# Dealing router steps and turns over other units of the 16-expert stages, and starting the second 8-expert stage's low rows earlier

## The chip, the cores and the metric

The kernel runs on one core of a Trainium2 chip. The metric is the device time of one execution in microseconds (us); the median of the runs is compared. Engines: PE (TensorE), DVE (VectorE), ACT (ScalarE), POOL (GpSimd), SP (SyncE, which here only issues DMAs).

## The reference

A stack of six blocks on a residual `x` of 8 sequences x 512 tokens x 128 features, float32:

```python
x = x + 0.5 * _L0_ffn_ref(_layernorm(x), ...)   # 8 experts, hidden 512, top 2
x = x + _L0_attn_ref(_layernorm(x), ...)        # 16 heads of 8
x = x + 0.5 * _L0_ffn_ref(_layernorm(x), ...)
x = x + 0.5 * _L1_ffn_ref(_layernorm(x), ...)   # 16 experts, width 64, top 2, and a shared one
x = x + _L1_attn_ref(_layernorm(x), ...)        # a state space block
x = x + 0.5 * _L1_ffn_ref(_layernorm(x), ...)
```

The part that matters here, the 16-expert block, is

```python
shared_out = silu(x @ shared_gate_w) * (x @ shared_up_w) @ shared_down_w
topk_probs, topk_idx = top_k(softmax(x_flat @ router_w), 2)
coeff = einsum('tk,tke->te', topk_probs, one_hot(topk_idx, 16))
for g, u, d, c in experts:
    acc = acc + (silu(x_flat @ g) * (x_flat @ u)) @ d * c[:, None]
```

The 8-expert block is a gelu layer pair per expert, weighed by the two largest probabilities of a softmax router.

## The kernel before, in words

Six phases run one after the other (`PHASES`: moe0, attn, moe0, moe1, ssm, moe1). There is no scheduler: each phase has one function per engine (`tensor`, `scalar`, `vector`, `gpsimd`, `sync`), and the order on an engine is the order in which that function issues. Engines meet by semaphores alone (`wait_ge`), and every engine runs its own instructions strictly in order, so an instruction that waits holds all behind it.

**The 16-expert stage** (`moe1_phase`). One body per sequence, `b` from `c0` to `end - 1`, eight in a stage. A body has nine units `j`: unit 0 is the shared expert, units 1 to 8 are pairs of routed experts. For a unit PE does two products of three matmuls each (`up1`, L1590 to L1592: high weights x high rows, high x low, low x high), ACT the silu (`silu1`, L1645), DVE the gate product (`gate1`, L1654 for unit 0 and L1657) and, four units later (`W_LAG`), the weighing with the token's coefficient (`weigh1`, L1666); PE's down product (`down1`, L1678) comes six units behind (`D_LAG`) and sums over the units in bank 6. Three units may be open between PE and DVE (`UPS`): PE starts a unit only when the gate three units back is done.

Beside the units a body prepares the next ones:

- the turn `norm_pe` (L231): PE transposes the normed rows of a later sequence into bank 7, and `norm_act` (L237) copies them to `xnT`; `xh_act` (L1596) and `xl_dve` (L1600) split `xnT` into high and low rows;
- the router: `router_pe` (L1507), then on DVE `router_a` (5 short operations, L1520 to L1525), `router_b` (7, L1533 to L1541) and `router_c` (7, L1549 to L1559), `router_b` and `router_c` each in two halves where the code wants them apart; ACT's `router_act` (tanh, L1512) stands between;
- the coefficients: `coef_pe` (L1565) transposes them into bank 7, `coef_act` (L1571) copies them to SBUF, and SP (`coef_sp`) stores them and loads them back repeated over 64 partitions, four loads of 512 KB, into one of two buffers;
- `arrive`: DVE brings sequence b + 2 up to date, by `combine` in the first stage (L313, eight operations: the routed rows of the 8-expert stage) and by a shorter update in the second (L3034); then `norm_a` (L204, L209) takes its statistics, POOL finishes them (`shift_pool`), and ACT writes the normed rows (`xn_act`, L1613);
- `back_pe` (L1692) transposes the sum of body b - 1 into bank 7 and `back_dve` (L1697) adds it to `x_res`.

Bank 7 is shared by turn, router, coefficients and `back_pe`; the turn at a body's end waits for L1697. The body `c0 + 1` differs: the coefficients of `c0` land late, so the down products of `c0` are made in its first units (`FIRST_DOWNS`, L1678) and DVE weighs two units of `c0` behind each of its first four gates.

**The second 8-expert stage** (`moe0_phase`, `occ` 1). The first sequence is computed densely, expert by expert: `i` is the expert, `c` one of four units (`up0` L950 to L952, `gelu0` L1014, `hh_act` L1024, `hl_dve` L1034, `down0`), `y_act`, `back_pe` (L1053) and `y_dve` (L1062, the weighed add to `x_res`) behind it; `back_pe(i)` needs `y_dve(i - 1)`. Meanwhile the last group of routed tokens gets its slots: `pick_a`, `pick_b` (L529 to L550), `group_pos` on PE, `group_copy` on ACT, `place_a`, `place_b` (L587 to L617), `place_c` (L626 to L636), `tables_dve`. The `route_last_*` functions say at which (i, c) each stands. The rows of the first sequence come split: `xh_act` (L895) and `xl_dve` (L900). Both ran at the stage's opening, behind the attention's last add `z_dve` (L2427), and `after_phases` held PE for that add.

## Time and profile before

| | us |
|---|---|
| median of 3 runs (1391.99 to 1400.24) | 1392.63 |
| the profiled execution | 1398.67 |
| its span on the core | 1396.9 |
| PE busy | 1236.2 (88%) |
| DVE busy | 1123.6 (80%) |
| ACT busy | 876.3 (63%) |
| POOL busy | 513.5 (37%) |

All times of rows are microseconds from the span's start. In the span the second 8-expert stage begins near 704, the first 16-expert stage near 897, its third body near 946, the second 16-expert stage near 1202. PE's busy share is an average over stages; what an edit is worth is read from who waits for whom inside a stage. PEclk is the granted TensorE clock as a share of the full 2.4 GHz.

### The profile page before, as it was taken

How to read it: one execution, taken by the hardware profiler on the slowest of the kernel's cores; microseconds unless marked ns; L12 is line 12 of the kernel's file. 1: busy time of each engine (PE TensorE's matmuls, PEld its weight loads, DVE VectorE, ACT ScalarE, POOL GpSimd, SP SyncE). 2: the span in 40 equal slices, each digit the busy share in tenths (PEclk: the TensorE clock that was granted, in tenths of full speed). 3: DMA queues.
4: the chain of work that ended last, by engine and by line, in shares of the span. 5: the costliest groups of instructions: out<-in, count | busy, mean ns of one | idle time of the engine just before them, and what ended most of it. 6: DMA issues, size and time to landing. Idle time of an engine off the chain costs nothing.

```text
span 1396.9 us, 22511 instructions
## 1 busy us (share of the span) xinstructions
PE 1236.2 (88%) x7168; PEld 783.7 (56%) x7168; DVE 1123.6 (80%) x2387; ACT 876.3 (63%) x1535; POOL 513.5 (37%) x762
## 2 busy tenths in 40 slices
PE   6768999678899879988888999899999899899998
PEld 5657989312222212322277999866666356666665
DVE  6865979789988989898677989877876787778785
ACT  5855777358887868877887777633333588333442
POOL 6772337543543506520363236605330320210100
PEclk9988999679998989999999999999999999999999
DMA  7495556522212202210253566456363010253534
GB/s 267 131 357 179 204 203 227 159 70 79 90 48 84 86 26 96 89 44 13 78 225 126 188 222 217 139 113 142 84 130 70 11 42 19 52 121 73 116 69 121
DMA packets 116608, 167.94 MB, mean 120 GB/s; under 512 B 18884, under 2 KB 63460, under 8 KB 115468
## 3 DMA queue, kind: packets, MB, share of 16 engines
q1 hardware_dynamic: 109324, 151.82, 36.7%
q0 software_dynamic: 7168, 14.69, 3.6%
q8 instruction: 58, 0.95, 0.3%
q14 instruction: 58, 0.48, 0.1%
HBM read 80.72 MB, written 45.09 MB: 90 GB/s over the span
## 4 chain that ended last, share of the span: by engine, by line
PE 53%; DVE 25%; issue 8%; ACT 7%; DMA 4%; POOL 2%; SPq 1%; DVEq 0%; ACTq 0%; POOLq 0%
PE bank L1678 6%; DVE shared L2297 6%; PE bank L2375 5%; PE pair L950 4%; PE pair L952 4%; PE pair L951 4%; PE pair L2357 3%; PE pair L1590 3%; PE pair L1592 3%; PE pair L1591 3%; PE pair L2289 3%; DVE shared L1034 3%; DMA shared<-p_coef_rows 2%; ACT shared L2365 2%; DVE shared L1032 2%
## 5 line engine op out<-in xcount | busy, mean ns | idle before, releaser
L2297 DVE TENSOR_REDUCE shared<-pair 128x2 f32<-128x1024 f32 x256 | 309.8, 1217 | 40.7 <-PE pair L2289 37.8
L2365 ACT ACTIVATE shared<-pair 128x1024 f32<-128x1024 f32 x256 | 260.5, 1021 | 51.1 <-PE pair L2357 49.5
L950 PE MATMUL pair<-shared 128*128 128x256 f32 (+1 forms) x704 | 228.0, 324 | 7.1 <-issue 3.6
L951 PE MATMUL pair<-shared 128*128 128x256 f32 (+1 forms) x704 | 218.2, 310 | 0.0
L952 PE MATMUL pair<-shared 128*128 128x256 f32 (+1 forms) x704 | 218.0, 310 | 0.0
L1034 DVE TENSOR_TENSOR shared<-shared 128x512 fp32r<-128x512 f32 x208 | 155.7, 757 | 59.9 <-ACT shared L1024 56.7
L1645 ACT ACTIVATE shared<-pair 128x512 f32<-128x512 f32 x144 | 85.7, 595 | 180.9 <-PE pair L1592 180.8
L1590 PE MATMUL pair<-shared 128*128 128x512 f32 x288 | 154.6, 537 | 4.9 <-DVE shared L1600 4.9
L1018 ACT ACTIVATE shared<-pair,shared 128x256 f32<-128x256 f32 x288 | 121.3, 476 | 49.9 <-PE pair L952 43.5
L950 PEld LDWEIGHTS pair<-shared 128*128 128x128 f32 x704 | 137.8, 196 | 14.9 <-issue 4.5
L2375 PE MATMUL bank<-shared 128*9 128x512 f32 x1024 | 138.8, 615 | 4.5 <-ACT shared L2365 4.3
L952 PEld LDWEIGHTS pair<-shared 128*128 128x128 f32 x704 | 137.9, 196 | 6.4
L1333 POOL CAST shared<-shared 128x1024 fp32r x72 | 81.6, 1134 | 161.7 <-PE pair L952 150.7
L951 PEld LDWEIGHTS pair<-shared 128*128 128x128 f32 x704 | 137.6, 196 | 5.4 <-issue 0.2
L649 POOL DMA_INDIRECT xs_rows<-shared,slots x112 | 117.6, 1050 | 55.5 <-issue 28.7
L281 POOL DMA_INDIRECT staged<-ys_rows,slots x112 | 116.3, 1039 | 57.1 <-ACT shared L2365 34.0
L1657 DVE TENSOR_TENSOR shared<-shared,pair 128x512 f32<-128x512 f32 x128 | 87.0, 682 | 58.6 <-ACT shared L1645 57.1
L1678 PE MATMUL bank<-shared,down_w 128*128 128x512 f32 x256 | 128.7, 595 | 1.6 <-DVE shared L1666 1.6
L2289 PE MATMUL pair<-shared 48*128 48x512 bf16 x512 | 104.2, 406 | 22.2 <-ACT shared L2365 10.5
L1592 PE MATMUL pair<-shared 128*128 128x512 f32 x288 | 115.4, 401 | 0.0
L1591 PE MATMUL pair<-shared 128*128 128x512 f32 x288 | 115.1, 400 | 0.0
L2357 PEld LDWEIGHTS pair<-shared 51*128 51x128 bf16 x512 | 24.7, 93 | 150.0 <-issue 88.6
(384 smaller groups left out, 2253.4 us busy)
## 6 DMA issues: line engine op xcount, KB each, us to landing
shared<-shared SPq DMA_DIRECT2D x144, 256.0 KB
shared<-p_coef_rows SPq DMA_DIRECT2D x64, 512.0 KB, 6.4
shared<-xs_rows SPq DMA_DIRECT2D x36, 256.0 KB, 3.0
ys_rows<-shared SPq DMA_DIRECT2D x36, 256.0 KB
w_keep<-shared SPq DMA_DIRECT2D x8, 1024.0 KB, 12.2
shared<-w_keep SPq DMA_DIRECT2D x16, 512.0 KB
shared<-p_q_parts SPq DMA_DIRECT2D x64, 96.0 KB, 2.3
shared<-p_k_parts SPq DMA_DIRECT2D x64, 96.0 KB, 2.4
```

What stands on the lines that cost most here:

```text
L950: nc.tensor.matmul(out_bank, w_hi, x_hi, start=start, stop=False)
L951: nc.tensor.matmul(out_bank, w_hi, x_lo, start=False, stop=False)
L952: return nc.tensor.matmul(out_bank, w_lo, x_hi, start=False, stop=stop)
L1034: nc.vector.tensor_tensor(hl[u % RING][:], hid[u % RING][:], hh[u % RING][:], ALU.subtract).then_inc(s["dve_done"], 1)
L1590: nc.tensor.matmul(out_bank, w_hi, x_hi, start=start, stop=False)
L1591: nc.tensor.matmul(out_bank, w_hi, x_lo, start=False, stop=False)
L1592: return nc.tensor.matmul(out_bank, w_lo, x_hi, start=False, stop=stop)
L1678: nc.tensor.matmul(bank[6][:], w, h, start=(j == 0), stop=(j == IT - 1)).then_inc(s["down_done"], 1)
L2289: last = nc.tensor.matmul(pair_of("max", b, m)[:, f, :], qa[par][rows, c, i * P:(i + 1) * P], ka[par][rows, c, :], start=True, stop=True)
L2297: nc.vector.tensor_reduce(mneg[:, i, 2 * c:2 * c + 2], pair_of("max", b, m)[:], AX_X, ALU.max, negate=True).then_inc(s["mx_read"], 1)
L2365: nc.scalar.activation(probs[st % 2][:, 2 * p:2 * p + 2, :], pair_of("exp", b, 2 * st + p)[:], ACT.Exp, scale=scale).then_inc(s["exp_done" ...
L2375: last = nc.tensor.matmul(bank[6][32 * hh:32 * hh + HD + 1, :], v_all[:, b * TILES + kt, hh % 2 * (H // 2) + g * HG // 2 + hh // 2, :], pr ...
```

## The change

It adds and removes no computation. Six moves:

1. Bodies from the third on: the turn `norm_pe`/`norm_act` goes from the end of body b - 1 (unit 8) and the head of body b to behind unit 1 of body b; the router matmuls from unit 0 to unit 2, `router_act` from 2 to 3, `router_a`, `router_b`, `router_c` from units 1, 2, 3 to 2, 3, 4.
2. The second body (`late`): everything of item 1 a unit later, except `router_c`, which stays at unit 4, now with `router_b`; `arrive` goes from unit 4 to unit 5.
3. First body: `router_b` and `router_c`, which stood together at unit 5, are dealt in halves to units 5, 6, 7, 8, and the low rows go from unit 7 to unit 6.
4. The coefficients of the second body are transposed and copied in its own unit 1 (on ACT ahead of that unit's silu) instead of at unit 8 of the first.
5. Second 8-expert stage: the low rows of the first sequence get a place in SBUF behind all others, and both halves of the split go into the attention's last steps: `xh_act` ahead of `ot_act`, `xl_dve` between `place_a` and `place_b`, ahead of `z_dve`. PE no longer calls `after_phases`.
6. Second 8-expert stage: the last group's slot work is dealt over units: `pick_a` (2,3), `pick_b` (3,0), positions (3,3), `place_a` in halves at (3,3) and (4,0), `place_b` in halves at (4,0) and (4,1), `place_c` in halves at (4,2) and (4,3).

The core of the diff:

```diff
             if occ:
                 w_all = view(P, NE0 * 4 * HID, F32R)
+                low_rows = view(P, T, F32R)
+            xl = [low_rows, low_more]
...
+            if occ:
+                dense_open.update(xh=lambda: xh_act(0), xl=lambda v: xl_dve(v, 0))
...
+            def last_group(v, G, at):
+                if at == (2, 3):
+                    pick_a(v, occ, G)
+                if at == (3, 0):
+                    pick_b(v, occ, G)
+                if at == (3, 3):
+                    place_a(v, occ, G, 0)
+                if at == (4, 0):
+                    place_a(v, occ, G, 1)
+                    place_b(v, occ, G, 0)
+                if at == (4, 1):
+                    place_b(v, occ, G, 1)
...
             def tensor(t):
-                after_phases(t, n)
                 f = base(n + 1)
                 if occ == 0:
+                    after_phases(t, n)
...
-                            if j == 8:
-                                coef_pe(b + 1)
                             continue
...
-                        if j == 1 and b == c0 + 1:
-                            nc.tensor.wait_ge(s["ct_sb"], b + 1)
+                        late = int(b == c0 + 1)
+                        if j == 1 and late:
+                            coef_pe(b)
+                        if j == 1 + late and ahead(b - 1):
+                            if b == c0 + 1:
+                                nc.tensor.wait_ge(s["ct_sb"], b + 1)
+                            else:
+                                nc.tensor.wait_ge(x_upd, u0 + b - 1)
                             norm_pe(f0 + b + 1)
-                        if j == (2 if b == c0 + 1 else 0) and b + 1 < end:
+                        if j == 2 + late and b + 1 < end:
                             router_pe(b + 1)
...
-                        if j == 8 and ahead(b):
-                            nc.tensor.wait_ge(x_upd, u0 + b)
-                            norm_pe(f0 + b + 2)
...
                         else:
-                            if j == 0 and b > c0 + 1 and ahead(b - 1):
-                                norm_act(f0 + b + 1, (b + 1) % 2)
+                            if j == 1 and b == c0 + 1:
+                                coef_act(b)
...
                             if j == 5:
-                                router_b(chain)
-                                router_c(v, b + 1, chain)
-                            if j == 7:
+                                router_b1(chain)
+                            if j == 6:
                                 xl_dve(v, b + 1)
+                                router_b2(chain)
+                            if j == 7:
+                                router_c1(v, b + 1, chain)
+                            if j == 8:
+                                router_c2(v, b + 1, chain)
...
-                        if j == (4 if b > c0 else 3) and b + 2 < end and not (mixed(n) and b == c0):
+                        if j == (4 if b > c0 + 1 else 5 if b > c0 else 3) and b + 2 < end and not (mixed(n) and b == c0):
                             arrive(v, b + 2 - c0)
```

The order of the changed kernel carries other line numbers: L1600, L1657, L1654, L1678, L1565 and L1590 of before are L1625, L1682, L1679, L1703, L1590 and L1615 in it.

DVE in the first body of a 16-expert stage, before, from the last router step of unit 5 to the first gate of the second body (`coef` holds the coefficients, `stats` and `mv` the statistics, L1600 writes the low rows):

```order
L1559 SCALAR_TENSOR_TENSOR coef<-rt_b,rt_m 128x64
L1657 TENSOR_TENSOR shared<-shared,pair 128x512
L204 BN_STATS stats<-x_res 128x6 x4
L209 BN_AGGR mv<-stats 128x2 x4
L1657 TENSOR_TENSOR shared<-shared,pair 128x512
L1600 TENSOR_TENSOR shared<-xnT,shared 128x512
L1657 TENSOR_TENSOR shared<-shared,pair 128x512
L1654 SCALAR_TENSOR_TENSOR shared<-shared,pair 128x512
```

and with the change, from unit 6's gate on:

```order
L1682 TENSOR_TENSOR shared<-shared,pair 128x512
L1625 TENSOR_TENSOR shared<-xnT,shared 128x512
L1563 TENSOR_TENSOR rt_a<-rt_a,first 128x64
L1564 TENSOR_REDUCE rt_n<-rt_a 128x4
L1565 TENSOR_TENSOR rt_a<-rt_a,rt_n 128x64
L1566 TENSOR_TENSOR rt_c<-rt_a,rt_c 128x64
L204 BN_STATS stats<-x_res 128x6 x4
L209 BN_AGGR mv<-stats 128x2 x4
L1682 TENSOR_TENSOR shared<-shared,pair 128x512
L1574 TENSOR_SCALAR rt_b<-rt_th 128x64
L1575 RECIPROCAL rt_b<-rt_b 128x64
L1576 SCALAR_TENSOR_TENSOR rt_b<-rt_th,rt_b 128x64
```

The low rows (L1600, now L1625) went from behind unit 7's gate to behind unit 6's, and the router steps that had all stood ahead of unit 6's gate now lie between the gates of units 6, 7 and 8.

PE at the seam of the second and third body, before: the last down product of the second, the turn (`xn`), unit 0 of the third, the router matmuls (`wr`, `xnT`) behind it.

```order
L1678 MATMUL bank<-shared,down_w 128x512
L231 MATMUL bank<-ident,xn 128x128 x4
L1590 MATMUL pair<-shared 128x512
L1591 MATMUL pair<-shared 128x512
L1592 MATMUL pair<-shared 128x512
L1590 MATMUL pair<-shared 128x512
L1591 MATMUL pair<-shared 128x512
L1592 MATMUL pair<-shared 128x512
L1678 MATMUL bank<-shared,down_w 128x512
L1507 MATMUL bank<-wr,xnT 128x16 x4
```

With the change, unit 1 of the third body with the down product ahead of it and behind it, and then the turn:

```order
L1703 MATMUL bank<-shared,down_w 128x512
L1615 MATMUL pair<-shared 128x512
L1616 MATMUL pair<-shared 128x512
L1617 MATMUL pair<-shared 128x512
L1615 MATMUL pair<-shared 128x512
L1616 MATMUL pair<-shared 128x512
L1617 MATMUL pair<-shared 128x512
L1703 MATMUL bank<-shared,down_w 128x512
L231 MATMUL bank<-ident,xn 128x128 x4
```

The turn left the body's end and stands two units later; the router matmuls follow another unit later.

DVE in the dense part of the second 8-expert stage, before, around the weighed add of the second expert (L1062):

```order
L616 TENSOR_REDUCE slot_f<-q_g 128x4
L617 CAST slots<-slot_f 128x8
L1034 TENSOR_TENSOR shared<-shared 128x512 x2
L626 SCALAR_TENSOR_TENSOR moved_e<-rest_e,jump_e 128x8
L627 TENSOR_TENSOR next_e<-next_e,pos_g 128x8
L628 TENSOR_TENSOR next_e<-next_e,moved_e 128x8
L629 SCALAR_TENSOR_TENSOR room_e<-blocks_e,rest_e 128x8
L632 TENSOR_TENSOR past_e<-upto_e,iota 128x288
L634 TENSOR_REDUCE ex_g<-past_e 128x36
L635 SCALAR_TENSOR_TENSOR ex_g<-ex_g 128x36
L636 TENSOR_TENSOR ex_all<-ex_all,ex_g 128x36
L1062 SCALAR_TENSOR_TENSOR x_res<-bank,w_dense,x_res 128x128 x4
```

and with the change:

```order
L1039 TENSOR_TENSOR shared<-shared 128x512
L626 SCALAR_TENSOR_TENSOR moved_e<-rest_e,jump_e 128x8
L627 TENSOR_TENSOR next_e<-next_e,pos_g 128x8
L628 TENSOR_TENSOR next_e<-next_e,moved_e 128x8
L629 SCALAR_TENSOR_TENSOR room_e<-blocks_e,rest_e 128x8
L1039 TENSOR_TENSOR shared<-shared 128x512
L632 TENSOR_TENSOR past_e<-upto_e,iota 128x288
L634 TENSOR_REDUCE ex_g<-past_e 128x36
L635 SCALAR_TENSOR_TENSOR ex_g<-ex_g 128x36
L636 TENSOR_TENSOR ex_all<-ex_all,ex_g 128x36
L1067 SCALAR_TENSOR_TENSOR x_res<-bank,w_dense,x_res 128x128 x4
L1039 TENSOR_TENSOR shared<-shared 128x512 x2
```

The low halves of two units now lie inside the slot work instead of beside it; the weighed add (now L1067) still comes behind all of it.

## Rows read from the trace of the kernel before

**Rows 1.** The page, its first line.

```profile
span 1396.9 us, 22511 instructions
```

**Rows 2.** Waits of PE, 896 to 1066: us in total, times, longest.

```profile
PE bank L231 <- DVE x_res L1697: 7.9, 5, 1.8
PE pair L1590 <- DVE shared L1600: 2.4, 1, 2.4
```

**Rows 3.** Busy time by stretch: PE, PEld, DVE, ACT, POOL, PEclk, DMA share, GB/s.

```profile
962.92:987.00 24.08, 22.55 (x93) 15.44 (x92) 19.50 (x56) 9.32 (x18) 10.69 (x12) 1.00 0.50 111
968.00:970.00 2.00, 0.47 (x3) 0.07 (x2) 1.40 (x3) 1.78 (x5) 1.63 (x2) 1.00 0.90 210
1224.00:1228.00 4.00, 3.88 (x10) 3.12 (x11) 0.95 (x3) 0.91 (x3) 1.16 (x2) 0.57 0.08 19
1268.62:1291.53 22.91, 22.56 (x93) 15.44 (x92) 18.36 (x51) 9.32 (x18) 2.04 (x4) 1.00 0.45 94
```

**Rows 4.** Order of time at two body seams, first 16-expert stage: start, us, engine.

```profile
945.88 0.63 PE L231 MATMUL bank<-ident,xn 128*128 128x128 f32 x4 [1.77 <-DVE x_res L1697]
...
966.32 0.68 DVE L1666 TENSOR_TENSOR shared<-shared 128x512 f32<-128x512 f32 x1
...
967.41 1.02 PE L1678 MATMUL bank<-shared,down_w 128*128 128x512 f32 x2
969.96 0.63 PE L231 MATMUL bank<-ident,xn 128*128 128x128 f32 x4 [1.53 <-DVE x_res L1697]
970.35 0.48 PE L1590 MATMUL pair<-shared 128*128 128x512 f32 x1
```

**Rows 5.** Order of time on DVE in the body that begins at 970.35.

```profile
972.63 0.69 DVE L1654 SCALAR_TENSOR_TENSOR shared<-shared,pair 128x512 f32<-128x512 f32 x1 [0.96 <-ACT shared L1645]
...
975.77 0.69 DVE L1657 TENSOR_TENSOR shared<-shared,pair 128x512 f32<-128x512 f32 x1 [1.85 <-ACT shared L1645]
...
985.01 2.31 DVE L313 SCALAR_TENSOR_TENSOR x_res<-staged,w_tok,x_res 128x128 f32<-128x128 f32 x8
```

**Rows 6.** First two bodies of that stage: DVE, ACT, PE in time; coefficient loads.

```profile
910.98 0.69 DVE L1657 TENSOR_TENSOR shared<-shared,pair 128x512 f32<-128x512 f32 x1 [0.51 <-ACT shared L1645]
...
916.11 0.57 ACT L1571 COPY shared<-bank 16x512 f32<-16x512 f32 x1 [0.23 <-PE bank L1565]
...
918.37 0.68 DVE L1657 TENSOR_TENSOR shared<-shared,pair 128x512 f32<-128x512 f32 x1
918.50 0.50 PE L1590 MATMUL pair<-shared 128*128 128x512 f32 x1 [2.43 <-DVE shared L1600]
...
921.45 1.28 DVE L1666 TENSOR_TENSOR shared<-shared 128x512 f32<-128x512 f32 x2
922.18 1.98 PE L1678 MATMUL bank<-shared,down_w 128*128 128x512 f32 x4 [0.63 <-DVE shared L1666]
922.25 0.58 ACT L1645 ACTIVATE shared<-pair 128x512 f32<-128x512 f32 x1
...
shared<-p_coef_rows SPq DMA_DIRECT2D x4, 512.0 KB, 6.1
```

**Rows 7.** Second 8-expert stage: PE, ACT and DVE in order of time.

```profile
703.74 0.47 PE L950 MATMUL pair<-shared 128*128 128x512 f32 x1 [2.67 <-DVE x_res L2427]
704.77 1.28 ACT L1014 ACT_TABLE_LOAD   x1 [4.50 <-PE pair L952]
...
724.32 0.18 DVE L529 TENSOR_REDUCE mx_g<-z_all 128x4 f32<-128x32 f32 x1
...
727.35 0.19 PE L508 MATMUL bank<-summed_g,ones_b 128*128 128x32 bf16 x1 [0.35 <-DVE summed_g L550]
...
738.73 1.13 DVE L1062 SCALAR_TENSOR_TENSOR x_res<-bank,w_dense,x_res 128x128 f32<-128x128 f32 x4
...
740.00 1.09 PE L1053 MATMUL bank<-ident,shared 128*128 128x128 f32 x4 [3.52 <-DVE x_res L1062]
```

59 lines of the change are left out of this document (34 added, 25 removed).

## The prediction

> **What bounds the kernel now.** I read the waits of TensorE (PE) stage by stage first, then PE's busy time in one body, then the order of time on PE, VectorE (DVE) and ScalarE (ACT) around each wait. In the first 16-expert stage the rows to see are five waits of PE for the residual add L1697, 7.9 us in all, and one of 2.4 us for the low rows L1600 [rows 2]. A steady body there lasts 24.08 us with PE busy 22.55; in the second 16-expert stage it lasts 22.91 with the same 22.56 busy [rows 3]. So PE is the bound in both, and the 1.5 us between them is the turn L231 at the body's end waiting for L1697: 1.53 us [rows 4]. DVE is busy 19.50 of 24.08, but in a lump: from unit 1's gate at 975.77, which still waited 1.85, it has no gap to the end of the combine at 987.32 [rows 5]. The second 8-expert stage starts at 703.74 after 2.67 us of waiting and loses 3.52 us at 740.00, where a transpose waits for the add L1062 that DVE reaches at 738.73 [rows 7].
>
> The profiled execution took 1398.67 us around its span of 1396.9 [rows 1], 6.0 over the median of 1392.63; I sum savings in the trace and take them off the median.
>
> **Steady bodies of the first 16-expert stage.** No instruction is added or removed; the turn goes behind unit 1 of the next body, so L1697 has some 4.5 us more, and the 1.53 goes. What is late next is DVE. Before, its lump begins with unit 1's gate, 975.77-970.35 = 5.42 us into the body. Now router part a goes with unit 2, b with 3, c with 4. Unit 2's gate can begin at 5.42 + 2.25 (a unit with its down product: 22.55 us over nine units, less turns and router) - 0.81 (router matmuls now behind it) + 0.39 (the turn now ahead) = 7.25. From there the old lump, less unit 1's gate and weighing (1.2), is 11.55-1.2 = 10.35, and unit 3's gate, which must wait for 7.25+2.25+0.81 = 10.31 while DVE is ready at 7.25+1.2+1.3 = 9.75, puts 0.55 into it: the combine ends at 18.15, not at 987.32-970.35 = 16.97. DVE is 1.2 us later for the weighings behind it. The tightest is the one at 966.32, ended 966.95, whose product PE began at 967.41 [rows 4]: slack 0.46, plus 0.39 because the turn now stands ahead of PE too, 0.85. So a wait of about 0.35 comes back: 24.08-1.53+0.35 = 22.9, a saving of 1.2 in each of four bodies (third to sixth), **4.8 us**. Bounds: nothing (the whole 1.5 comes back) to 1.55 a body, 6.2.
>
> **First two bodies of that stage.** Before, DVE does router parts b and c in one piece after unit 5's gate (910.98), so that the low rows end late and PE's second body starts at 918.50, after 2.43 [rows 6]. Now the low rows stand right behind unit 6's gate, near 913, and this wait goes. But all that DVE had to do before unit 8's gate (918.37) is still to be done, c2 now behind it. The second body's first gate comes at 918.37+0.65 = 919.0 and its first weighing at 919.6, 1.85 before the old 921.45. PE's down product, which began 0.73 behind that weighing (922.18), begins at 920.35: the 2.4 has moved there, and 1.85 is won. Next, on ACT the coefficient copy is now queued ahead of unit 1's silu, and on PE the coefficient transposes stand behind two down products (1.7): they end at 922.45, the copy at 923.2, the silu starts then, where it was 922.25 before, and the next weighing is ready for PE at 923.2+0.6+0.6+0.75 = 925.15. PE has done unit 2 by 922.45+1.45 = 923.9 and waits 1.25: 0.6 of the gain is left. From 925.15 PE needs two downs, turn, unit 3, two downs, router, unit 4 (7.5 us) and the silu 0.85, so unit 4's gate is at 933.5. Behind it DVE now has b and c together (3.7), gate and weighing (1.2), combine (2.3), statistics (1.3), gate and weighing (1.2): 943.2, ready for PE some 0.7 later, 943.9. PE has come to that product at 942.5 and waits 1.4. It ends near 944.8, and the third body starts there without the turn that began at 945.88 before [rows 4]: **1.1 us** won. Bounds: -3 (the three waits of 2.4, 1.3 and 1.4 hold and each also loses clock) to +4.8 (2.4, 0.6 and 1.8, all gone). I take the path just worked, since each wait in it is read from neighbours.
>
> The coefficients of the second body leave 6.5 us later than before (copy 916.11, now 922.7). The four loads land 6.1 us after issue [rows 6]; with the store before them that is some 9 to 13 us, so 932 to 936, and their first user runs after 937: hidden, with 1 us to spare.
>
> **The second 16-expert stage.** The same two bodies, with a 1.2 us update in place of the combine. The same steps give PE's first down product at 1225.9 (before 1229.06), then waits of 1.3 and 0.4, and the third body 2.4 us earlier; of this 1.5 is clock, since behind its 2.42 us wait the granted clock was 0.57 for 4 us [rows 3], the 1.2 GHz level for much of it. The four steady bodies can fall only from 22.91 to some 22.5, DVE having 1.1 us less to do: 1.6. Together **4.0 us**, bounds 0 and 7.
>
> **The second 8-expert stage.** PE no longer waits for the attention's last add; low rows written between the two halves of slot work let it start near 701.1. But ACT still waits for that add, which the low rows push 0.7 later, to 703.65, so the first gelu (table load at 704.77 before) comes 1.1 earlier, not 2.6. Downstream DVE decides. Its pick (724.32 before) starts 2.1 earlier, with one unit less ahead of it: PE now meets its result one unit sooner and waits there some 1.5 (0.35 before). From the pick to L1062 at 738.73 [rows 7] DVE had almost no gap, and dealing the same instructions out removes none: the add ends 0.75 earlier. The early start is thus swallowed at 740: **0.75 us**. Bounds: -0.7 (the add later by the low rows) and +6.6 (2.7, 3.5 and 0.4). The reloads of weights start 0.7 later and stay ahead of use.
>
> **Sum.** 4.8 + 1.1 + 4.0 + 0.75 = 10.65. 1392.63 - 10.65 = 1382.0 us, 0.76% less. A measurement of this kernel tells about 1% (13.9 us) from no change.
>
> **Rivals.**
> *All the named waits go and nothing takes their place.* 11.3 in the first 16-expert stage, 5 and 1.5 of clock in the second, 6.7 in the 8-expert one: 24.5, so 1368.1. For it: DVE and ACT have room on average. Against: DVE's lump is continuous just where the waits are [rows 5, 6].
> *The wait comes back in the steady bodies.* If DVE's slack is half a microsecond smaller than I read, each steady body of the first stage keeps 1.2 to 1.5 as waits on weighings; only the rest is won: 1392.63 - 5.85 = 1386.8. For it: the combine, statistics and weighings stand in a row. Against: DVE has 24.08 - 19.50 = 4.6 us of gaps in a body [rows 3] to catch up.
> *The clock falls: slower than before.* Waits of PE that were one per body become several short ones, in four steady bodies and three in each second body: ten. Behind 2.42 us of waiting the clock was 0.57 for 4 us, which cost 1.7 [rows 3]. Ten times that is 17, against 10.65: 1399. It decides from seven of the ten on. Against: behind 1.53 us waits the clock stayed at 1.00, the 2.4 GHz level, in the stretch 968 to 970 too [rows 3].
> The Trainium skill ("TensorE: Matmul & The Clock Gate", section "A second HAM failure mode: psum-queue depth-cycling") says that frequent short idles between groups of matmuls can make the clock swing between its levels. By it this rival would hold and the time be near 1399; the trace has short idles at full clock, so it gets little.
> *The change does nothing it says.* Excluded for the turn, which moves in every body; for the 8-expert stage it is my own forecast, nearly.
>
> **How the numbers follow.** Forecast, with a few microseconds either way (1377 to 1386): 0.52. Steady waits back (1384 to 1390): 0.20. All waits gone or mostly (1366 to 1377): 0.23. Clock: 0.05. Leaving out one in ten at either end, 1372 to 1389. Faster by over 1% needs 13.9 us: the 0.23 and a little of the forecast's edge, 0.26. Slower by over 1%: 0.02. Within: 0.72.
>
> **What would show it.** In the changed profile the turn L231 waits nowhere; steady bodies of the first stage last 22.9, with down products waiting 0.3 to 0.5 for weighings; in each second body PE waits 2.3 for the first weighing, about 1.3 for the third, 1.4 (0.4 in the second stage) for the last; in the 8-expert stage a wait of 1.5 at the group positions and one of 2.8 for L1062's successor, ending near 739. It would be wrong if the second body's waits were missing, if the steady body lasted over 23.5, or if the 8-expert stage gained over 2 us.

## The result, and the profile after

| | before | changed |
|---|---|---|
| median of six runs, us | 1395.64 (1391.99 to 1400.24) | 1382.64 (1379.44 to 1385.08) |
| ratio, 95% interval | | 0.9918 (0.9895 to 0.994) |
| profiled execution's span, us | 1396.9 | 1379.8 |

The change makes the kernel 0.82% faster, and the whole interval lies below 1; the forecast was 0.76%. The spans differ by more than the medians, 17.1 us. Of these, 5.5 lie ahead of the change, in stages that it does not touch: the attention's output product starts at 699.93 in the trace before and at 694.47 in the changed one, and in a later run with those stages unaltered too (the 16-expert parts alone) at 695.18. So the two traces are compared stage by stage, each from its own first mark: A from the attention's output product to the coefficient transposes of the first 16-expert stage (it holds the second 8-expert stage), B from there to that stage's last transposes back (L1717, before L1692), S the state-space stage up to the next coefficient transposes, C from there to the last transposes back.

| us | A | B | S | C |
|---|---|---|---|---|
| before | 197.3 | 195.0 | 117.3 | 183.2 |
| changed | 194.1 | 189.3 | 118.3 | 179.5 |
| gained | 3.2 | 5.7 | -1.0 | 3.7 |
| forecast | 0.75 | 5.9 | 0 | 4.0 |

The sum is 11.7, beside 11.4 by the ratio and 13.0 by the medians.

One caution for B. PE runs unaltered code in the stage's first units, but its granted clock over the first 5 us was 0.50 in the trace before and 0.71 in the changed one. The kernel with the 16-expert parts alone, below, started at 0.50 as well and took 190.5 us in B. So at the same starting clock B gains 4.5, and 1.2 of the 5.7 is that clock.

The waits of TensorE in the changed kernel, first for 890 to 1066 (it answers to [rows 2]), then for 1190 to the end:

```profile
PE bank L1703 <- DVE shared L1691: 4.5, 3, 2.1
...
PE bank L1703 <- DVE shared L1691: 3.5, 3, 2.1
PE bank L1590 <- DVE coef L1584: 1.6, 1, 1.6
PE bank L1717 <- ACT shared L1707: 0.7, 1, 0.7
```

The turn L231 no longer waits for the residual add, and the 2.4 us for the low rows is gone. In their place stand waits of the down product L1703 (L1678 before) for the weighing L1691: three in the second body of the first stage, two in that of the second stage (2.08 and 1.08; the third counted in that line, 0.29, is at the stage's very last products). The wait for the coefficients L1584, 1.6, ends just where C begins and so is counted in S. Busy time in the body that begins at each turn, two of the first 16-expert stage and one of the second, to be read beside [rows 3]:

```profile
939.66:962.83 23.17, 23.07 (x94) 15.39 (x92) 19.41 (x55) 9.20 (x18) 10.31 (x12) 1.00 0.49 105
962.83:985.99 23.16, 23.05 (x93) 15.39 (x92) 19.41 (x55) 9.20 (x18) 10.30 (x12) 1.00 0.53 118
...
1263.26:1285.67 22.41, 22.41 (x94) 15.53 (x93) 18.34 (x51) 9.20 (x18) 2.03 (x4) 1.00 0.47 101
```

A body went from 24.08 to 23.16 and from 22.91 to 22.41. The busy column misleads here: PE shows 23.05 busy of 23.16, though its work is the same 22.41 as in the second stage. A matmul's end is modelled, and a short wait hides under it. What shows such waits is the weight load's row (PEld), which names whom it waited for, and the distance of each matmul from the body's start, laid beside the same matmul of the stage without waits:

```profile
974.23 2.31 DVE L313 SCALAR_TENSOR_TENSOR x_res<-staged,w_tok,x_res 128x128 f32<-128x128 f32 x8
976.57 0.69 DVE L1682 TENSOR_TENSOR shared<-shared,pair 128x512 f32<-128x512 f32 x1
977.18 0.68 DVE L1691 TENSOR_TENSOR shared<-shared 128x512 f32<-128x512 f32 x1
977.91 0.30 PEld L1703 LDWEIGHTS bank<-shared,down_w 128*128 128x128 f32 x2 [0.34 <-DVE shared L1691]
980.35 0.30 PEld L1703 LDWEIGHTS bank<-shared,down_w 128*128 128x128 f32 x2 [0.37 <-DVE shared L1691]
980.96 0.19 PEld L1615 LDWEIGHTS pair<-shared 128*128 128x128 f32 x1 [0.31 <-DVE shared L1625]
981.52 1.65 ACT L1638 ACTIVATE xn<-x_res,shift,rs_y 128x128 f32<-128x128 f32 x4 [3.52 <-POOL shift L1632]
983.08 1.06 ACT L1670 ACTIVATE shared<-pair 128x512 f32<-128x512 f32 x2
985.03 0.30 PEld L1703 LDWEIGHTS bank<-shared,down_w 128*128 128x128 f32 x2 [0.34 <-DVE shared L1691]
```

Against the second stage's body, PE falls behind by 0.38 us at the weighing behind the combine (977.91), by 0.10 and 0.14 at 980.35 and at the low rows (980.96), and, after 0.05 is made up, by 0.18 from 985.03 on: 0.75 in all, the whole difference of 23.16 and 22.41.

The second body of the first 16-expert stage, in order of time (answers to [rows 6]):

```profile
908.83 0.68 DVE L1679 SCALAR_TENSOR_TENSOR shared<-shared,pair 128x512 f32<-128x512 f32 x1
909.42 1.28 DVE L1691 TENSOR_TENSOR shared<-shared 128x512 f32<-128x512 f32 x2
910.16 1.98 PE L1703 MATMUL bank<-shared,down_w 128*128 128x512 f32 x4 [2.07 <-DVE shared L1691]
...
911.98 0.60 PE L1590 MATMUL bank<-ident,coef 128*16 128x128 f32 x4
...
912.62 0.58 ACT L1596 COPY shared<-bank 16x512 f32<-16x512 f32 x1 [2.96 <-PE bank L1590]
913.10 0.58 ACT L1670 ACTIVATE shared<-pair 128x512 f32<-128x512 f32 x1
...
914.32 1.29 DVE L1691 TENSOR_TENSOR shared<-shared 128x512 f32<-128x512 f32 x2
915.06 1.12 PE L1703 MATMUL bank<-shared,down_w 128*128 128x512 f32 x2 [1.10 <-DVE shared L1691]
...
934.04 0.70 PE L1703 MATMUL bank<-shared,down_w 128*128 128x512 f32 x1 [1.30 <-DVE shared L1691]
```

These are the three waits that were forecast as 2.3, 1.3 and 1.4: the first weighing behind VectorE's lag, the third behind the silu that is queued after the coefficient copy, the last behind router, combine and statistics. In the second stage the third of them shows only in the weight load's row, and PE falls behind by 0.46 us there:

```profile
1235.25 0.30 PEld L1703 LDWEIGHTS bank<-shared,down_w 128*128 128x128 f32 x2 [0.57 <-DVE shared L1691]
```

The second 8-expert stage (answers to [rows 7]):

```profile
695.36 0.48 PE L955 MATMUL pair<-shared 128*128 128x512 f32 x1
...
696.40 1.28 ACT L1019 ACT_TABLE_LOAD   x1 [2.07 <-PE pair L957]
...
697.37 0.69 DVE L2456 TENSOR_TENSOR x_res<-bank,shared 128x512 f32<-128x512 f32 x1
...
698.09 1.27 ACT L1019 ACTIVATE shared<-pair,vecs 128x512 f32<-128x512 f32 x2 [0.41 <-DVE x_res L2456]
...
718.86 0.19 PE L508 MATMUL bank<-summed_g,ones_b 128*128 128x32 bf16 x1 [1.26 <-DVE summed_g L550]
...
731.09 1.13 DVE L1067 SCALAR_TENSOR_TENSOR x_res<-bank,w_dense,x_res 128x128 f32<-128x128 f32 x4
732.36 0.63 PE L1058 MATMUL bank<-ident,shared 128*128 128x128 f32 x4 [2.48 <-DVE x_res L1067]
```

From the attention's output product the first gelu is 3.62 us away (698.09 - 694.47), before it was 6.14; the stall at L1058 ends 37.9 us away, before 40.1. It lasts 2.48 instead of 3.52, and the wait at the group positions grew from 0.35 to 1.26.

### The profile page after: what moved, and what is told of

The parts are those of the page before. It is cut to its first block, busy times and chain, and to the rows that moved or that the text cites. A ratio compares the mean times of both kernels' runs of the same rounds, so it can differ in the third digit from the quotient of the medians.

```text
span 1379.8 us, 22519 instructions
## 1 busy us (share of the span) xinstructions
PE 1227.8 (89%) x7168; PEld 776.2 (56%) x7168; DVE 1120.5 (81%) x2387; ACT 875.9 (63%) x1535; POOL 511.8 (37%) x762
## 4 chain that ended last, share of the span: by engine, by line
PE 54%; DVE 25%; issue 8%; ACT 8%; POOL 3%; DMA 2%; SPq 0%; DVEq 0%; ACTq 0%; POOLq 0%
PE bank L1703 8%; DVE shared L2326 6%; PE bank L2404 5%; PE pair L1615 4%; PE pair L1617 4%; PE pair L1616 3%; PE pair L955 3%; PE pair L957 3%; PE pair L2386 3%; PE pair L956 3%; PE pair L2318 3%; DVE shared L1039 3%; ACT shared L2394 2%; POOL xs_rows L649 2%; DVE shared L1037 2%
## 5 line engine op out<-in xcount | busy, mean ns | idle before, releaser
L2326 DVE TENSOR_REDUCE shared<-pair 128x2 f32<-128x1024 f32 x256 | 309.9, 1217 | 37.9 <-PE pair L2318 34.8
L955 PE MATMUL pair<-shared 128*128 128x256 f32 (+1 forms) x704 | 225.5, 320 | 6.8 <-issue 3.6
L957 PE MATMUL pair<-shared 128*128 128x256 f32 (+1 forms) x704 | 215.9, 307 | 0.0
L956 PE MATMUL pair<-shared 128*128 128x256 f32 (+1 forms) x704 | 215.6, 306 | 0.0
L1615 PE MATMUL pair<-shared 128*128 128x512 f32 x288 | 152.4, 529 | 0.2 <-DVE shared L1625 0.2
L955 PEld LDWEIGHTS pair<-shared 128*128 128x128 f32 x704 | 136.0, 193 | 15.0 <-issue 5.4
L1682 DVE TENSOR_TENSOR shared<-shared,pair 128x512 f32<-128x512 f32 x128 | 87.2, 682 | 65.9 <-ACT shared L1670 64.8
L957 PEld LDWEIGHTS pair<-shared 128*128 128x128 f32 x704 | 135.8, 193 | 5.9
L956 PEld LDWEIGHTS pair<-shared 128*128 128x128 f32 x704 | 135.7, 193 | 4.9 <-issue 0.2
L1703 PE MATMUL bank<-shared,down_w 128*128 128x512 f32 x256 | 130.4, 601 | 8.8 <-DVE shared L1691 8.2
L649 POOL DMA_INDIRECT xs_rows<-shared,slots x112 | 117.6, 1050 | 51.4 <-issue 28.9
L2318 PE MATMUL pair<-shared 48*128 48x512 bf16 x512 | 103.6, 403 | 22.5 <-ACT shared L2394 10.8
L1617 PE MATMUL pair<-shared 128*128 128x512 f32 x288 | 114.2, 397 | 0.0
L1616 PE MATMUL pair<-shared 128*128 128x512 f32 x288 | 113.7, 395 | 0.0
```

Source lines behind the costliest of these rows:

```text
L649: g.indirect_dma_start(out=xs_rows, out_offset=bass.IndirectOffsetOnAxis(ap=slots[:, t, k:k + 1], axis=0), in_=xn_rows[occ][:, t, :], in_o ...
L955: nc.tensor.matmul(out_bank, w_hi, x_hi, start=start, stop=False)
L956: nc.tensor.matmul(out_bank, w_hi, x_lo, start=False, stop=False)
L957: return nc.tensor.matmul(out_bank, w_lo, x_hi, start=False, stop=stop)
L1615: nc.tensor.matmul(out_bank, w_hi, x_hi, start=start, stop=False)
L1616: nc.tensor.matmul(out_bank, w_hi, x_lo, start=False, stop=False)
```

## The experiments

Stage lengths of all profiled runs, beside the medians; the last two columns are the granted clock over the first 4 us of A and the first 5 us of B (before: 1.00 and 0.50; changed: 1.00 and 0.71). Kernels of one group of lines shared their runs of the kernel before.

| kernel | median us | ratio to before | A | B | S | C | clock, A | clock, B |
|---|---|---|---|---|---|---|---|---|
| 8-expert part alone | 1389.59 | 0.9964 (0.9946 to 0.9982) | 193.9 | 194.8 | 117.0 | 182.7 | 1.00 | 0.70 |
| 16-expert parts alone | 1385.63 | 0.9942 (0.9922 to 0.9962) | 198.1 | 190.5 | 117.4 | 179.5 | 0.77 | 0.50 |
| early low rows alone | 1392.49 | 0.9992 (0.9972 to 1.0012) | 197.1 | 196.4 | 117.3 | 183.1 | 0.57 | 0.66 |
| low rows twice | 1384.77 | 0.994 (0.9916 to 0.9964) | 194.0 | 189.9 | 118.3 | 179.6 | 1.00 | 0.72 |
| | | | | | | | | |
| dealing alone | 1392.63 | 0.9984 (0.9965 to 1.0003) | 197.2 | 194.8 | 117.0 | 182.7 | 0.80 | 0.68 |
| low rows earlier | 1384.36 | 0.9934 (0.991 to 0.9957) | 194.6 | 190.5 | 117.1 | 179.5 | 1.00 | 0.53 |
| down products later | 1373.62 | 0.986 (0.9834 to 0.9887) | 194.5 | 185.9 | 114.1 | 176.2 | 1.00 | 0.51 |
| silu first | 1379.02 | 0.9887 (0.9863 to 0.9911) | 195.4 | 189.0 | 114.3 | 178.1 | 1.00 | 0.50 |
| | | | | | | | | |
| second body, three parts | 1376.51 | 0.9895 (0.9876 to 0.9914) | 194.8 | 184.7 | 117.0 | 175.7 | 0.54 | 0.66 |
| norm later | 1383.82 | 0.9936 (0.991 to 0.9961) | 194.1 | 188.4 | 117.2 | 179.6 | 1.00 | 0.72 |
| both | 1372.33 | 0.986 (0.9841 to 0.9879) | 194.1 | 183.5 | 117.6 | 175.8 | 1.00 | 0.71 |
| changed kernel again | 1381.08 | 0.9942 (0.9921 to 0.9963) | 195.2 | 189.3 | 118.3 | 179.5 | 0.57 | 0.72 |

**The two halves of the change.** The kernel before with the 8-expert part of the diff alone, then with the 16-expert part alone.

> The kernel before with the two parts of the change in the second 8-expert stage alone (low rows' home and early low rows, slot work dealt out); the 16-expert stages are as before. Theory (the stage's gain is its own and lasts): from the attention's last product to the 16-expert stage's coefficient transposes 3.2 us less than in the kernel before, its median 3 us lower, ratio 0.9977. Rival (the prediction's own step: the add on VectorE decides and swallows the early start, what the changed profile showed was the clock's luck): 0.75 us less.

> The kernel before with the change of the two 16-expert stages alone. Theory (the parts add up): first 16-expert stage 5.7 us shorter, second 3.8 us shorter, as in the changed kernel, median some 8.5 to 9.5 us lower, ratio 0.9936, since the 8-expert stage's 3.2 is missing. Rival (the parts lean on each other, for instance through the low rows' home or the time at which weights arrive): either stage differs from the changed kernel's by more than 1 us.

Measured: A 193.9 with the first, 198.1 without it (before: 197.3). B and C are 190.5 and 179.5 with the second, and B is 1.2 longer than in the changed kernel. That 1.2 arises in the stage's first 10 us, where PE runs unaltered code: the granted clock over the first 5 was 0.50 in this run, as in the kernel before, and 0.71 in the changed kernel's. The steady bodies are 23.17 and 22.41 as there. The ratios multiply to 0.9906, beside 0.9918 for the whole. So the parts add up, and the 8-expert part wins over 3 us, not 0.75; the rival of the first run falls, and that of the second is met by its number (over 1 us in B) but by the clock, not by the parts leaning on each other.

**Which half of the 8-expert part.** Early low rows alone:

```diff
-                dense_open["xT"] = xT_dense
+                dense_open.update(xT=xT_dense)
...
+                dense_open.update(xh=lambda: xh_act(0), xl=lambda v: xl_dve(v, 0))
```

with the low rows' own home, the calls in the attention's end and PE's entry without its wait as in the change; the last group's steps stay where they were.

> The kernel before with the early low rows (and their own home) alone; pick, placing and group positions of the last group stay in one piece and at their old units. Theory: the first up product comes 2.9 us earlier, the clock does not fall at 705, and the gain is kept but for what the undealt placing costs: 2 to 2.6 of the 3.2 us. Rival (the prediction's: VectorE's work up to the residual add decides, and only dealing could move it): the stall after that add grows from 3.5 us to 5.5, 0.75 us or less is won.

Then the dealing alone, low rows left behind the attention's add. (PE's call of `after_phases` is gone in this kernel too. PE then waits for the low rows instead, and its first product stands where it stood, 3.75 us behind the attention's output product against 3.81 before.)

> The kernel before with the dealing of the last group's slot work in the second 8-expert stage alone; low rows where they were. In the trace from the attention's last product to the 16-expert stage's coefficients the kernel before takes 197.3 us (198.1 in the run with the 16-expert parts alone), with low rows alone 197.1, with both parts 193.9. Theory (the dealing is what pays: it takes VectorE's work out from before the residual add, whose stall goes from 3.5 to 2.5, and the low rows only hand on their start): some 195.5. Rival (neither pays alone; the start of 2.9 us and the dealing are needed together): 197 or more. Rival of the prediction (dealing the same instructions out moves nothing): 197.3 and the stall at 3.5.

A is 197.1 and 197.2, where both together give 193.9 to 195.4 in ten profiles and neither gives 197.3 and 198.1 in two. By these figures neither pays alone, but they can't be laid side by side as they are. The stalls of PE at the transposes behind the weighed add, with low rows alone and with the dealing alone, each followed by the ten microseconds behind it (busy times, granted clock third from the right):

```profile
733.71 1.09 PE L1058 MATMUL bank<-ident,shared 128*128 128x128 f32 x4 [3.56 <-DVE x_res L1067]
...
733.71:743.71 10.00, 10.00 (x38) 8.02 (x39) 4.77 (x13) 3.98 (x7) 4.46 (x5) 0.71 0.28 89
```

```profile
735.79 0.63 PE L1053 MATMUL bank<-ident,shared 128*128 128x128 f32 x4 [2.45 <-DVE x_res L1062]
...
735.79:745.79 10.00, 9.66 (x50) 7.62 (x51) 5.67 (x14) 6.62 (x12) 4.53 (x5) 1.00 0.29 93
```

The clock at A's start differs too. Here is the first stretch of A with low rows alone, and of the changed kernel's second profile (the last run below), whose code there is the changed kernel's:

```profile
695.07:699.07 4.00, 4.00 (x15) 3.56 (x16) 3.66 (x15) 0.57 (x1) 3.08 (x4) 0.57 0.18 59
```

```profile
692.35:696.35 4.00, 4.00 (x15) 3.57 (x16) 3.66 (x15) 0.57 (x1) 3.08 (x4) 0.57 0.18 59
```

The changed kernel's first profile had 1.00 there. Its first gelu stood 3.62 us behind the attention's product, in the second profile 4.72, and A came out at 194.1 and 195.2: 1.1 us by the starting clock alone. Without the early low rows the low starting clock costs 0.7 (gelu at 6.14 in the kernel before, at 6.8 with the 16-expert parts alone and with the dealing alone). Among the five profiles that started low, neither edit gives 198.1, the dealing 197.2, the low rows 197.1, both 195.2 and 194.8. So each edit alone is worth 0.9 to 1.0 there.

The low rows' 197.1 holds one thing more. From the stall's end to the coefficients 158.4 us pass, against 157.2 and 157.4 in the two profiles with neither edit, whose stall was as long (3.52 and 3.49). In that stretch PE waits 0.50 and 0.54 us for loads of weights and 0.27 for GpSimd, which neither of those two profiles shows; the kernel with the silu first, which has both edits, shows 0.43 and 0.26 of the same kind and is 1.2 longer there than the changed kernel. Taking off 1.1 for the starting clock and 1.1 for these waits, an estimate from the rows just named, low rows alone would stand near 194.9 and win 2.4, as their first text said; the dealing alone, less 0.7, near 196.5 and win 0.8. With one profile of each this is an estimate and not shown (a wait for weights alone need not lengthen the stretch: the dealing alone has one of 1.20 and passed it in 156.1), and the medians (ratios 0.9992 and 0.9984, each within 0.2% either way) can't decide it. (This kernel's B, 1.4 us over that of the kernel before, is unaltered code as well: the clock behind its waits of 2.43 and 1.77 us there was 0.63 and 0.57 over 4 us, where the kernel before kept 1.00.)

What the changed kernel's own trace shows against the kernel before, both at a starting clock of 1.00, is firmer. The first gelu comes 2.5 sooner. The dealing costs VectorE 0.35 (0.5 sooner to the pick, 0.85 later to the add), so the add begins at 36.6 instead of 38.8. From the stall's end to the coefficients 156.2 us pass instead of 157.2, 1.1 less when not rounded; 0.6 of it is there ten microseconds behind the stall, where the clocks differ. Dealing alone had 156.1 behind a stall of 2.45. With low rows alone the rival's stall of 5.5 us did not come; it stayed at 3.56.

**Is VectorE's lump the bound of a steady body?** One subtraction more, 0.60 us of VectorE's time where it follows another, in each steady body:

```diff
+            spare = view(P, T, F32R)
...
                             if j == 6:
+                                if not late:
+                                    nc.vector.tensor_tensor(spare[:], xnT[(b + 1) % 2][:], xh[(b + 1) % 2][:], ALU.subtract)
                                 xl_dve(v, b + 1)
```

> The changed kernel with one more VectorE subtraction of 128x512 (0.68 us, into a spare buffer that nobody reads) ahead of the low rows in the third and later bodies of both 16-expert stages. Theory (VectorE's lump from unit 2's gate to the residual add sets what a steady body loses over 22.4): first stage's steady body 23.16 -> 23.8, second stage's 22.41 -> 22.7, the time 4 us over the changed kernel, about 1386.5. Rival (PE and its queue set the body, VectorE having 3.8 us of gaps in each): bodies 23.16 and 22.41 as they are, time 1382.6.

Measured: 23.32 and 22.41. For the first stage both texts were wrong; the second stage is as the rival said. The 0.6 appeared in full where it was put,

```profile
980.98 0.69 DVE L1870 TENSOR_TENSOR shared<-xnT,shared 128x512 fp32r<-128x512 f32 x1
981.58 0.68 DVE L1626 TENSOR_TENSOR shared<-xnT,shared 128x512 fp32r<-128x512 f32 x1
982.31 0.19 PEld L1616 LDWEIGHTS pair<-shared 128*128 128x128 f32 x1 [0.90 <-DVE shared L1626]
```

but the next body's first products then waited for the low rows and nothing behind them did: at the body's end PE had lost its time in one place instead of two, and the body grew by 0.15. In the second stage the slack took all of it.

**The low rows earlier, and the norm behind the silu.** First the low rows alone, in the third and later bodies:

```diff
                             if j == 2 + late:
                                 chain = router_a(v, b + 1)
+                                if not late:
+                                    xl_dve(v, b + 1)
...
-                            if j == 6:
+                            if j == 6 and late:
                                 xl_dve(v, b + 1)
```

> The changed kernel with the low rows of the next body made behind router part a (unit 2) instead of behind unit 6's weighing, in the third and later bodies. Doubling that subtraction lengthened the first 16-expert stage's steady body from 23.16 to 23.31 only. Theory (the wait of 0.14 us at the next body's first unit, and the late gates behind it, go; the 0.38 behind the combine stays): body 22.9, second stage 22.4 as it is, time 1 us below the changed kernel, not to be told from it by the median. Rival (the lump's whole length counts): body 22.5, 2.6 us less.

Measured: 23.24, not 22.9 nor 22.5. The wait for the low rows went; a longer one came at unit 8:

```profile
979.83 1.65 ACT L1638 ACTIVATE xn<-x_res,shift,rs_y 128x128 f32<-128x128 f32 x4 [3.53 <-POOL shift L1632]
...
981.38 1.06 ACT L1670 ACTIVATE shared<-pair 128x512 f32<-128x512 f32 x2
981.99 0.69 DVE L1682 TENSOR_TENSOR shared<-shared,pair 128x512 f32<-128x512 f32 x1 [1.65 <-ACT shared L1670]
...
983.40 0.30 PEld L1703 LDWEIGHTS bank<-shared,down_w 128*128 128x128 f32 x2 [0.49 <-DVE shared L1691]
```

VectorE now stands idle for 1.65 us, so it is not VectorE: ScalarE applies the norm (1.65 us, behind GpSimd's factors), and two units' silus are queued behind that. A second chain was next, from the statistics over GpSimd and ScalarE back to VectorE. The next kernel adds

```diff
-                        if j == 7 and b > c0 and ahead(b):
+                        if j == (8 if b > c0 + 1 else 7) and b > c0 and ahead(b):
                             xn_act(f0 + b + 2, (b + 2 - c0) % B)
```

> The changed kernel with, in the third and later bodies, the low rows early (behind router part a) and ScalarE's application of the norm behind unit 8's silu instead of ahead of it. With the low rows early alone the steady body went from 23.16 to 23.25: the wait for them went, and 0.22 and 0.10 us came at unit 8's weighing, behind the chain statistics, GpSimd's factors, norm on ScalarE, silu, gate. Theory (that chain is the second bound of the body): with the silu ahead of the norm these waits go, the body is 22.8 in the first stage and 22.4 in the second. Rival (the norm then comes too late for the turn behind the next body's unit 1, or the combine alone sets the body): the turn waits, or the body stays at 23.1 to 23.3.

Measured: 22.93 and 22.41; the turn did not wait. The theory holds in kind, at 22.93 for 22.8: the two waits behind the norm are gone. What is left against the second stage's body is 0.3 us at the weighing behind the combine and 0.2 at the next one.

**The second body.** Down products of the first body one unit later:

```diff
-            FIRST_DOWNS = ((), (-8, -7), (-6, -5), (-4, -3), (-2,), (-1,))
+            FIRST_DOWNS = ((), (), (-8, -7), (-6, -5), (-4, -3), (-2, -1))
```

> The changed kernel with the first body's down products in the second body one unit later on PE (units 2 to 5 instead of 1 to 5), so that unit 2's up products run where PE waits 2.1 us for the first weighing. Theory (PE only meets VectorE's lag at a bad place; another unit's work covers it, 1.4 of the 2.1 goes, the 1.1 behind it as well): second body shorter by 1.5 to 2.5 us in each 16-expert stage, time 3 to 5 us below the changed kernel. Rival (VectorE decides downstream; what is won early comes back as a longer wait at unit 5's weighing, now 1.3 us): less than 0.5 us a stage.

and in another kernel ScalarE's copy behind the silu:

```diff
-                            if j == 1 and b == c0 + 1:
-                                coef_act(b)
...
                         silu1(b, j)
+                        if j == 1 and b == c0 + 1:
+                            coef_act(b)
```

> The changed kernel with ScalarE's copy of the second body's coefficients behind unit 1's silu instead of ahead of it, in both 16-expert stages. The prediction said that the silu queued behind that copy makes PE wait 1.3 us at the third weighing (measured 1.1). Theory: this wait goes, in each stage, and the second body is 0.5 to 1 us shorter, time 1 to 2 us below the changed kernel. Rival (the wait is swallowed at unit 5's weighing, which waits that much longer): 0 to 0.3 us.

With the later down products B is 3.4 and C 3.2 us shorter, over the theory's 1.5 to 2.5, and all three waits are gone. What PE still waits for at the start of B is this (885 to 960), the second line belonging to the stage before:

```profile
PE bank L1590 <- DVE coef L1584: 0.9, 1, 0.9
PE bank L1590 <- DVE shared L1074: 0.8, 1, 0.8
```

With the silu first, the way from the second body's coefficient transposes to the third's fell from 16.08 to 14.73 us, and from 16.07 to 14.73 in the second stage: the whole wait of 1.1 and a little more, and nothing swallowed it (B as a whole shows 0.3, because the clock at its start was 0.50 against 0.71). Then both, with the transposes and the copy behind unit 2:

```diff
+                        if j == 2 and b == c0 + 1:
+                            coef_pe(b)
                         for t_ in FIRST_DOWNS[j] if b == c0 + 1 and j < D_LAG else (j - D_LAG,):
...
-                        if j == 1 and late:
-                            coef_pe(b)
...
                         silu1(b, j)
+                        if j == 2 and b == c0 + 1:
+                            coef_act(b)
```

> The changed kernel with three things in the second body: down products one unit later on PE (as in the run before, which won 3.4 and 3.2 us in the two 16-expert stages), the coefficient transposes behind unit 2 instead of unit 1, where they waited 0.9 us for VectorE, and ScalarE's copy of them behind unit 2's silu. The coefficients leave 1.5 to 2 us later and have 6 us of slack. Theory (those 0.9 us are the last wait of the second body and nothing queues behind them): stages 4.3 and 4.1 us shorter than in the changed kernel, with no wait of PE in the second body. Rival (VectorE's steps up to unit 5 decide by now): 3.4 and 3.2 as before, with a wait at a later weighing.

> Both variants together: the second body's and the steady bodies'. Theory (the two places are independent): the stages are shorter by the sum of the two, some 5.5 and 4.1 us against the changed kernel, and the time is the lowest of all, 1371 to 1374. Rival (the gain of the second body depends on when the later bodies start): the sum falls short by over 1 us.

> The changed kernel itself, unaltered, beside the variants. In the state-space stage, which no kernel here alters, the changed kernel took 118.3 us between the last product of the first 16-expert stage and the coefficients of the second, five others 117.0 to 118.3, and two variants 114.1 and 114.3, where the granted clock stayed at 1.00 in the stage's first 20 us. Theory (whether the clock dips there hangs on the run): another profile of the same kernel may well show 114. Rival (it hangs on what PE did in the stage before): 117 to 118.3 again. For the time: 1382.6 by the theory that this is the same kernel.

The second body has no wait left; B is 4.7 and C 3.7 shorter (expected 4.3 and 4.1). Its median is 2.9 us above that of the kernel with the later down products alone, although B and C together are 1.8 shorter; in the traces it took 2.9 more in S. Together with the steady bodies' variant B is 5.8 and C 3.7 shorter (expected 5.5 and 4.1), so the two places are independent. That kernel took 1372.33 us, 8.75 below the changed kernel in the same series (1381.08) and 1.4% below the kernel before; the one with the later down products alone has the same ratio, 0.986, with 3.2 us of it in S, where nothing was altered. The waits left from 1185 to the end in the combined kernel: the first ends where C begins and is counted in S, the other two are at the end of C, behind the last body.

```profile
PE bank L1590 <- DVE coef L1584: 1.8, 1, 1.8
PE bank L1717 <- ACT shared L1707: 0.7, 1, 0.7
PE bank L1703 <- DVE shared L1691: 0.3, 1, 0.3
```

The changed kernel again took 118.3 us in S, as its rival said, and 1381.08 for 1382.6.

Differences of 1 us between stages are read from traces; the medians of these series scatter by 2 to 3 us around them (the norm later: a stage shorter by 1.0, a median higher by 2.7 than the changed kernel's beside it).

## Why the prediction was right, and where it was not

The time, 1382.0 for 1382.6, is closer than its sum. The traces give 3.7 for 4.8 in the steady bodies, 2.0 for 1.1 in the first bodies, 3.7 for 4.0 in the second 16-expert stage, 3.2 for 0.75 in the 8-expert stage, and a loss of 1.0 in S that was not in the sum: 11.7 for 10.65. The mechanisms of both 16-expert stages held; that the misses cancel to 1 us is luck. So is the base, in part: the forecast was taken from a median of 1392.63, and the six runs beside the result gave 1395.64.

*What bounds the kernel.* Right: PE in both stages, the wait at L231 in between. But 22.55 of busy time was taken for the floor of a body; the floor is 22.41.

*Steady bodies, first stage: 1.2 us forecast, 0.92 measured, four times.* The mechanism was right: the turn's wait went and VectorE's later lump brought part of it back. The term mis-sized is what comes back: one wait of 0.35 was forecast, and four places add up to 0.75. The floor under it, 22.41 and not 22.55, made good 0.14 of this. The place was wrong too. The step worked out the slack of the weighing at 966.32, after the combine's end; the first to be late is the one right behind the combine, and the last loss comes through a chain that the step never named, statistics, GpSimd, norm on ScalarE, silu. The runs with the low rows earlier and the norm later show that chain: 23.24, then 22.93.

*First two bodies: 1.1 forecast, 2.0 measured* (65.7 to 63.7 us from the first to the fourth coefficient transposes, the third body's head among them). Waits 2.07, 1.10 and 1.30 for 2.3, 1.3 and 1.4: the path was right, and each wait a little shorter than worked out, 0.5 in all. The rest of the surplus is not of the path. The kernel with the 16-expert parts alone, which began the stage at the clock of the kernel before (0.50), took 64.9 us for the same stretch, a gain of 0.8; the changed kernel began at 0.71, which gives the other 1.2. At the same clock the term was thus 0.3 too high. The coefficient loads stayed hidden: those of the second body land 7.8 us after issue instead of 6.1, and no weighing waited for them. That the middle wait comes from ScalarE's queue is shown by the kernel with the silu first.

*Second 16-expert stage: 4.0 forecast, 3.7 measured.* First bodies 1.8 for 2.4, with waits of 2.08 and 1.08 us and the third, forecast as 0.4, at 0.46; steady bodies 0.49 each, 2.0 for 1.6.

*Second 8-expert stage: 0.75 forecast, 3.2 measured.* Two steps failed. The first: "ACT still waits for that add [...] so the first gelu (table load at 704.77 before) comes 1.1 earlier, not 2.6". It came 2.5 earlier. The step put the table load of 1.28 us behind the add; it went out at 696.40, 1.66 us before the add ended at 698.06, as soon as PE's first products let it (1.03 behind PE's start in both traces), and only the gelu waited. The second: the clock was left out. Behind the stall of 3.5 us at 740 it was 0.86 over ten microseconds; the dealing shortened that stall to 2.5, and the clock behind it was 1.00: with what follows, 1.1 us up to the coefficients. What the text said of the dealing itself, that it takes nothing from VectorE, was right, and 0.35 too kind. "The early start is thus swallowed at 740" fails with the first step: the stall ends 2.2 us earlier behind the attention's product than before (37.9 against 40.1), and in the kernel with the early low rows alone 1.4 earlier, at the lower starting clock. The text named a gain of over 2 us here as a sign that it would be wrong, and it was.

*The rivals.* All waits gone (1368): no, but the experiments reach 1372 by taking away just the waits that were forecast, so they were real and not a law of the kernel. Steady waits back: no, half of them. The clock falls: no. The granted clock is 1.00 over the first stage's steady bodies, and over 906 to 920, with two of the waits in it:

```profile
906.00:920.00 14.00, 10.83 (x41) 6.13 (x40) 8.67 (x19) 5.60 (x11) 1.76 (x4) 1.00 0.37 84
```

By the Trainium skill ("TensorE: Matmul & The Clock Gate", section "A second HAM failure mode: psum-queue depth-cycling") frequent short idles could have made it swing. In the changed kernel and in the eight others with its 16-expert parts the waits of 2.1 us and below inside those stages left it up. But the length of a wait does not settle it. The wait of 2.43 us for the low rows stands in the first 16-expert stage of the kernel before and of the kernel with the 8-expert part alone, whose code there is the same, and this is what followed:

```profile
918.50:922.50 4.00, 3.37 (x13) 2.47 (x14) 2.21 (x4) 2.29 (x6) 1.29 (x3) 1.00 0.48 128
```

```profile
909.04:913.04 4.00, 4.00 (x11) 3.14 (x12) 1.07 (x2) 1.15 (x3) 1.29 (x3) 0.57 0.24 76
```

The wait of 1.77 us at the seam of second and third body was followed by 1.00 in three kernels with the old 16-expert code and by 0.57 over 4 us in the fourth, early low rows alone. So this rival had more behind it than the prediction's row 968 to 970 lets one see.

## What to carry to other kernels

When an engine meets another's lag at a known place, ask first what independent work of its own can stand there: one unit of up products moved ahead of the waiting down products won more (6.6 us) than the steady bodies' whole repair. A moved wait has more than one successor, so look for the second chain, through the small engines, before pricing what comes back. And a wait can cost twice, once as time and once as clock behind it; shortening a long one may be worth more than its length says. Before two traces are compared by the microsecond, compare the granted clock at the start of the stretch: in A and in B it alone made 1.1 and 1.2 us between profiles of the same code.

## What the runs showed that was not expected

The table load is not held by what holds its gelu: it ran for 1.28 us from 696.40, and the add on which the gelu waited ended at 698.06.

The clock behind waits: over the ten microseconds from the end of the 3.5 us stall in the 8-expert stage it was 0.86, 0.71 and 0.71 in three profiles; behind 2.5 us at the same place it was 1.00 in nine and 0.83 in two (low rows earlier, later down products). The shorter stall is followed by a lost clock more rarely, not never.

The state-space stage is altered by no kernel, yet takes 114.1 to 118.3 us. Its clock in the 12 us from 6 us after the last transposes back, in the changed kernel, the changed kernel again, and the kernels with later down products and with the silu first:

```profile
1083.86:1095.86 12.00, 9.46 (x20) 4.05 (x20) 8.95 (x32) 8.39 (x19) 4.24 (x7) 0.72 0.00 0
```

```profile
1082.82:1094.82 12.00, 9.45 (x20) 4.05 (x20) 8.96 (x32) 8.42 (x19) 4.25 (x7) 0.72 0.00 0
```

```profile
1078.22:1090.22 12.00, 8.55 (x25) 4.02 (x26) 9.86 (x36) 9.67 (x22) 5.18 (x7) 1.00 0.02 6
```

```profile
1086.22:1098.22 12.00, 8.54 (x25) 4.03 (x26) 9.85 (x36) 9.67 (x22) 5.18 (x7) 1.00 0.02 5
```

The same kernel twice gave the same 0.72 and the same 118.3 us. That is two profiles, and it does not exclude chance from run to run: the same two differed in the clock at A's start, 1.00 and 0.57. PE's order of work in the 100 us before is the same in all four, and the fully combined kernel had 1.00 here, lost clock later in the stage and took 117.6. What decides it stays open. It matters for reading small changes: the medians put the kernel with later down products 9 us below the changed one, and its profile has 4.2 us of its gain in S.
